# An edge gather and scatter-add: gathers ahead of the scatters paced by memsets, sums written into the rows they came from

## The chip, the cores and the metric

The kernel runs on one core of a Trainium2 chip. The metric is the device time of one execution in microseconds (us); the time before is the median of three runs. The profile is that of one further execution.

The engines are called by the short names of the profile: PE (TensorE matmul) and PEld (its weight load), DVE (VectorE), ACT (ScalarE), POOL (GpSimd, which here also issues every indirect DMA) and SP (SyncE, which here only issues DMAs). Times inside the profile count from the span's start.

## The reference

There are 100000 nodes of 128 float32 features, and 25000 edges, sorted by `dst`. The kernel adds to every node what its outgoing edges carry:

```
h   = maximum(layernorm(x), 0)
deg = number of edges with that src          (segment_sum of ones over src)
deg_inv = where(deg > 0, rsqrt(deg), 0)
for each edge e:  row = src[e], col = dst[e]
    norm   = deg_inv[row] * deg_inv[col]
    msg[e] = sum over b of comps[type[e], b] * (h[col] @ bases[b])     b = 0..3
    msg[e] = msg[e] * alpha[type[e]] * norm
out = x + segment_sum(msg, row)
```

## The kernel before

The edges are padded to 196 tiles of 128 edges, in 49 groups of 4 tiles. A tile's 128 gathered rows of x (one for each edge's `dst`) take `row(t)`, a [128, 128] float32 piece of the tensor `rows`, which has room for all 196 tiles. All orders are written out by hand; each engine has one instruction stream, and semaphores tie them.

- **Copy.** `out` must first be x. `copy` moves x to `out` in 50 pieces of 1 MB, two in flight, 4 from ACT's queue and 46 from SP's. Scatters add into `out`, so POOL waits for all of the copy before the first one.
- **Histogram.** PE counts the degrees with one-hot matmuls over the 196 tiles (L723); DVE makes the one-hots (L458, L459).
- **Looks.** For each tile PE looks up both degrees (`look`, L737, 8 matmuls), and DVE picks them out (`pick`, L481). DVE makes the one-hots for it in `turned_hots` (L475) from `edge_row`, a ring of broadcast rows that ACT's queue (at first SP's) loads.
- **Gathers.** `gather(t)` (L372) is an indirect DMA issued by POOL. ACT takes each group's mean and squares in `stats(g)` (L595 to L603), which waits for the landing of the group's four gathers.
- **Main loop,** 49 steps k of one group each. PE multiplies (L756), ACT takes the first of four terms (`first`, L641), DVE adds the other three (`combine`, L518), the last of which writes the message over `row(t)`.
- **Sums.** `add_same(t)` (PE, L764 and L766) adds up the messages of the same `src` inside a tile, and takes in what the tile before carries over. ACT evacuates it in `keep_sum(t)` (L651) into `acc`, a ring of 6 buffers.
- **Scatters.** POOL adds `acc` to `out` with an indirect DMA with add (L393). Scatter t waits for `keep_sum(t)` and for the landing of scatter t-2.

Three couplings matter for the change. `keep_sum(t)` waits until scatter t-6 has landed, because the ring has 6 buffers. `stats` at the end of step k goes as far as gathers that stand, in POOL's stream, ahead of the scatter `sums_until(k - 1)`; and `norms_in` on DVE needs the stats. POOL's stream itself is in this order:

1. gathers 0 to 55, each waiting for a share of the histogram;
2. gathers 56 to 107 (`FIRST_GATHERS` is 108), each waiting for a look or a product of PE (`pace`);
3. the wait for the copy;
4. the 196 scatters, with gathers 108 to 195 between them, seven to every ten scatters.

Sums are made in step k up to `sums_until(k)`, which is 5 (k - 2) up to step 10 and 4 k after it: in step 39 the sums 152 to 155, in step 42 the sums 164 to 167.

Of the kernel before, what the change touches and what calls it, by code (L numbers as in the profile page):

```python
# [5 lines left out]
ALU = mybir.AluOpType  # L6
ACT = mybir.ActivationFunctionType
# [6 lines left out]
P = 128  # L14
GROUP = 4
# [8 lines left out]
def build(nc, x, src, dst, edge_type, bases, comps, alpha, out):  # L24
    N, D = x.shape
    E = src.shape[0]
    R, B = comps.shape
    TILES = -(-E // P)
# [21 lines left out]
    FIRST_LOOK = 3  # L50
# [11 lines left out]
    TYPE_AT = [TILES - 1 - (TYPE_TILES - 1) * (TYPE_PARTS - 1 - i) for i in range(TYPE_PARTS)]  # L62
    TW = TYPE_TILES * P

    EDGE_RING = 4
    HOT_RING = 6
    TYPE_RING = 4
    SAME_RING = 3 * BATCH
    PART_RING = 7
    ACC_RING = 6  # L70


    def look_until(step):
# [6 lines left out]

    SUM_STEP, SUM_RATE = 3, 5


    HIST_GATHERS = 56
    LOOK_GATHERS = HIST_GATHERS + 4 * FIRST_LOOK * GROUP // 3
    FIRST_GATHERS = LOOK_GATHERS + 3 * GROUP * SUM_STEP


    def gathers_until(t):
        return min(TILES, FIRST_GATHERS + (7 * t + 9) // 10)  # L90

    def sums_until(step):
        return min(TILES, GROUP * max(0, step), max(0, step - SUM_STEP + 1) * SUM_RATE)
# [12 lines left out]
    def stats_until(step):  # L106
        return min(STATS_BEFORE + 2 * (step + 1), gathers_until(sums_until(step - 1)) // GROUP)
# [15 lines left out]
    with ExitStack() as ctx:  # L123
        def sb(name, shape, dt=F32):
            return ctx.enter_context(nc.sbuf_tensor(name, shape, dt))

        def sem(name):
            return ctx.enter_context(nc.semaphore(name))
# [24 lines left out]
        def row(t):  # L153
            return rows[:, t * D:(t + 1) * D]
# [27 lines left out]
        table = table_bits[:].bitcast(F16)  # L182
        edge_row = sb("edge_row", [P, EDGE_RING, 2, W], F16)
        turned_hot = sb("turned_hot", [P, 2, CHUNKS, 2 * W], F16)
# [23 lines left out]
        carried = sb("carried", [P, 2, BATCH])  # L208
        sum_scale = sb("sum_scale", [P, TILES])
        scatter_idx = sb("scatter_idx", [P, TILES], I32)  # L210
        acc = sb("acc", [P, ACC_RING, D])

        pst = ctx.enter_context(nc.psum_tensor("pst", [P, 8, BANK], F32))
        LOOK, TURNED, SUMS, PRODUCT = 0, 2, 3, 4
# [14 lines left out]
        row_table_ready = sem("row_table_ready")  # L229
        rows_stored = sem("rows_stored")  # L230
        idx_ready = sem("idx_ready")
        type_row_loaded = [sem(f"type_row_loaded{b}") for b in range(TYPE_RING)]
        edge_row_loaded = [sem(f"edge_row_loaded{r}") for r in range(EDGE_RING)]
        src_row_loaded = [sem(f"src_row_loaded{b}") for b in range(2)]
# [8 lines left out]
        look_ps = sem("look_ps")  # L243
# [11 lines left out]
        product_ready = sem("product_ready")  # L255
# [8 lines left out]
        scattered = [sem(f"scattered{b}") for b in range(2)]  # L264
# [9 lines left out]
        def load_edge_row(engine, g):  # L274
            if g >= EDGE_RING:
                engine.wait_ge(turned_hot_ready, g - EDGE_RING + 1)
            engine.dma_start(edge_row[:, g % EDGE_RING, :, :],
                             rows16_dram[0:2, g * W:(g + 1) * W].rearrange("(o k) e -> o k e", o=1)
                             .to_broadcast([P, 2, W])).then_inc(edge_row_loaded[g % EDGE_RING], 16)

# [58 lines left out]
        @block.gpsimd  # L339
        def _(pool):  # L340
            pool.iota(iota_i[:], [[1, CHUNKS * P]], base=0, channel_multiplier=0).then_inc(iota_ready, 1)
            pool.iota(chunk_i[:], [[P, CHUNKS]], base=0, channel_multiplier=1).then_inc(iota_ready, 1)
            pool.iota(spare_i[:], [[P, GROUP]], base=SPARE, channel_multiplier=1).then_inc(iota_ready, 1)
            pool.memset(ident[:], 0.0).then_inc(ident_cleared, 1)
            pool.memset(later[:, 0:P], 1.0).then_inc(ident_cleared, 1)
            pool.memset(later[:, P:2 * P], 1.0 / ONE).then_inc(ident_ready, 1)
            pool.wait_ge(ident_cleared, 2)
            pool.affine_select(out=ident[:], in_=ident[:], compare_op=ALU.not_equal, fill=1.0, base=0,
                               pattern=[[-1, P]], channel_multiplier=1).then_inc(ident_ready, 1)
            pool.affine_select(out=later[:, 0:P], in_=later[:, 0:P], compare_op=ALU.is_ge, fill=0.0, base=0,  # L350
                               pattern=[[1, P]], channel_multiplier=-1).then_inc(ident_ready, 1)

            def pace(t):
                if 0 < t < HIST_GATHERS:
                    pool.wait_ge(hot_used, t * TILES // HIST_GATHERS)
                elif HIST_GATHERS <= t < LOOK_GATHERS:
                    pool.wait_ge(look_ps, (t - HIST_GATHERS) * FIRST_LOOK * GROUP // (LOOK_GATHERS - HIST_GATHERS) + 1)
                elif LOOK_GATHERS <= t < FIRST_GATHERS:
                    tile, part = divmod(t - LOOK_GATHERS, 3)
                    if part == 0:  # L360
                        pool.wait_ge(product_ready, tile + 1)
                    else:
                        pool.wait_ge(look_ps, FIRST_LOOK * GROUP + 2 * tile + part)

            def gather(t):
                g = t // GROUP
                pace(t)
                if t == EARLY_TILE:
                    pool.wait_ge(hot_used, TILES)
                    pool.wait_ge(coef_ps, TYPE_PARTS)  # L370
                    pool.wait_ge(rows_stored, 16 * 4)
                pool.indirect_dma_start(row(t), None, x,  # L372
                                        bass.IndirectOffsetOnAxis(ap=dst_i[:, t:t + 1], axis=0)) \
                    .then_inc(row_gathered[g], 16)

            pool.wait_ge(idx_ready, 1)
            for t in range(FIRST_GATHERS):
                gather(t)
            gathered = FIRST_GATHERS

            pool.wait_ge(spare_filled, 16)
            for b in range(COPY_RING):
                pool.wait_ge(copied[b], 16 * (COPIES // COPY_RING))
            for t in range(TILES):
                for u in range(gathered, gathers_until(t)):
                    gather(u)
                gathered = gathers_until(t)
                if t % BATCH == 0:
                    pool.wait_ge(scatter_ready, t // BATCH + 1)
                if t >= 2:  # L390
                    pool.wait_ge(scattered[t % 2], 16 * (t // 2))
                pool.wait_ge(acc_ready, t + 1)
                pool.indirect_dma_start(out, bass.IndirectOffsetOnAxis(ap=scatter_idx[:, t:t + 1], axis=0),  # L393
                                        acc[:, t % ACC_RING, :], None, compute_op=ALU.add) \
                    .then_inc(scattered[t % 2], 16)

        @block.vector
# [192 lines left out]
        def _(act):  # L590
# [53 lines left out]
            def keep_sum(t):  # L644
                if t % BATCH == 0:
                    act.wait_ge(scatter_ready, t // BATCH + 1)
                act.wait_ge(sums_ps, t + 1)
                if t >= ACC_RING:
                    u = t - ACC_RING
                    act.wait_ge(scattered[u % 2], 16 * (u // 2 + 1))  # L650
                act.activation(acc[:, t % ACC_RING, :], pst[:, SUMS, 0:D], ACT.Copy, scale=sum_scale[:, t:t + 1]) \  # L651
                    .then_inc(acc_ready, 1)

            act.wait_ge(padded, 3)
# [41 lines left out]
            for t in range(sums_until(GROUPS - 1), TILES):  # L696
                keep_sum(t)

        @block.tensor
        def _(pe):  # L700
# [18 lines left out]
            for t in range(TILES):  # L719
                b = t % HOT_RING  # L720
                pe.wait_ge(hot_ready, t + 1)
                for c in range(CHUNKS):
                    last = pe.matmul(pst[:, HIST + c, 0:LO], hots[:, b, c * P:(c + 1) * P], hots[:, b, CHUNKS * P:],  # L723
                                     start=(t == 0), stop=(t == TILES - 1))
# [34 lines left out]
            def add_same(t):  # L759
                pe.wait_ge(same_ready, t + 1)  # L760
                pe.wait_ge(message_ready, t + 1)
                if t >= 1:
                    pe.wait_ge(acc_ready, t)
                last = pe.matmul(pst[:, SUMS, 0:D], same[:, t % SAME_RING, 0:P], row(t), start=True, stop=(t == 0))  # L764
                if t >= 1:
                    last = pe.matmul(pst[:, SUMS, 0:D], same[:, (t - 1) % SAME_RING, P:2 * P],  # L766
                                     acc[:, (t - 1) % ACC_RING, :], start=False, stop=True)
                last.then_inc(sums_ps, 1)

            pe.wait_ge(table_ready, CHUNKS)  # L770
# [5 lines left out]
            for k in range(GROUPS):  # L776
                if k + 1 < GROUPS:
                    turn(k + 1)
                for j in range(GROUP):
                    multiply(k * GROUP + j)  # L780
                    todo = sums_at(k, j)
                    for t in todo[:1]:
                        add_same(t)
                    for t in looks_at(k, j):
                        look(t)
                    for t in todo[1:]:
                        add_same(t)
            for t in range(sums_until(GROUPS - 1), TILES):
                add_same(t)
# [24 lines left out]
```

## Time and profile before

| | us |
|---|---|
| median of 3 runs (753.51 to 755.52) | 754.39 |
| the profiled execution | 752.15 |
| its span, first to last instruction | 750.2 |
| POOL busy | 540.3 |
| DVE busy | 596.4 |
| PE busy | 574.7 |
| ACT busy | 370.1 |

The span is 2 us shorter than the profiled execution's own time, and that one is 2.2 us under the median. The page cuts the span into 40 equal slices of 18.75 us and gives each engine's busy share in tenths. A row of the waits gives the idle time of an engine before a line, what ended it, how often, and the longest. Idle time of an engine that bounds nothing costs nothing.

### The profile page before, as it was taken

The page shows a single profiled execution, that of the slowest core. Times are in us where ns is not written, and L with a number is a line of the kernel's source. Part 1 is how long each engine was busy: PE and PEld are TensorE (multiplying, and loading weights), DVE is VectorE, ACT ScalarE, POOL GpSimd, SP SyncE. Part 2 cuts the span into 40 slices and gives each one's busy share as a digit, 9 for nine tenths or more (in the row PEclk, how much of TensorE's full clock was granted, in tenths as well). Part 3 has the DMA queues.
Part 4 walks back from the last instruction along what each step waited for, and adds up shares of the span by engine and source line. Part 5 has one row for each costly group of instructions (what it writes and reads, how often), then busy time and mean ns, then how long its engine had stood idle before and what let it go on. Part 6 is the DMA issues. An engine that isn't in the chain of part 4 may idle for free.

```text
span 750.2 us, 13642 instructions
## 1 busy us (share of the span) xinstructions
PE 574.7 (77%) x3922; PEld 406.0 (54%) x3922; DVE 596.4 (80%) x2624; ACT 370.1 (49%) x1494; POOL 540.3 (72%) x404
## 2 busy tenths in 40 slices
PE   4999985665676876987778788886797878888860
PEld 4666654443454645655556565655565656665430
DVE  7999995466775676886987899986998999998730
ACT  0345542244424678664545655645656534446530
POOL 3788886455555587778788888878878767767775
PEclk9999998687788899999998999999999999999995
DMA  8999999989833335444535455444455545544332
GB/s 272 287 326 339 331 361 323 319 296 327 307 101 81 70 54 122 79 92 69 109 52 100 92 86 95 96 81 95 82 95 96 92 78 78 86 57 82 35 36 25
DMA packets 56574, 108.89 MB, mean 145 GB/s; under 512 B 9339, under 2 KB 48264, under 8 KB 55684
## 3 DMA queue, kind: packets, MB, share of 16 engines
q0 software_dynamic: 34496, 25.72, 25.6%
q1 hardware_dynamic: 4416, 50.68, 18.7%
q10 hardware_dynamic: 17588, 31.62, 13.5%
q8 instruction: 32, 0.52, 0.3%
q14 instruction: 42, 0.34, 0.1%
HBM read 94.89 MB, written 64.61 MB: 213 GB/s over the span
## 4 chain that ended last, share of the span: by engine, by line
DVE 14%; DMA 13%; issue 10%; PE 9%; POOL 8%; ACT 7%; ACTq 0%; POOLq 0%
DMA out_dram<-acc,scatter_idx 11%; POOL out_dram L393 6%; DVE masked L481 4%; DVE part_sum L518 4%; PE pst L756 3%; PE pst L737 3%; DVE turned_hot L475 2%; POOL rows L372 2%; DVE same L537 2%; ACT acc L651 2%; DMA rows<-in_x_dram,dst_i 2%; DVE rows L518 2%; ACT scratch L603 2%; PE pst L764 1%; ACT scratch L595 1%
## 5 line engine op out<-in xcount | busy, mean ns | idle before, releaser
L393 POOL DMA_INDIRECT out_dram<-acc,scatter_idx x196 | 313.8, 1601 | 106.3 <-issue 53.7
L372 POOL DMA_INDIRECT rows<-in_x_dram,dst_i x196 | 224.4, 1145 | 96.4 <-issue 36.2
L737 PE MATMUL pst<-table_bits,turned_hot 128*128 128x198 f16 x1568 | 183.1, 267 | 84.0 <-DVE masked L481 61.1
L756 PE MATMUL pst<-bases_sb,h_turned 128*128 128x512 f32 x392 | 214.1, 629 | 0.0
L737 PEld LDWEIGHTS pst<-table_bits,turned_hot 128*128 128x128 f16 x1568 | 147.3, 105 | 113.6 <-issue 59.1
L518 DVE SCALAR_TENSOR_TENSOR part_sum<-pst,coef,part_sum 128x128 f32<-128x128 f32 x392 | 115.7, 343 | 96.2 <-ACT part_sum L641 89.3
L764 PEld LDWEIGHTS pst<-rows,same 128*128 128x128 f32 x392 | 73.0, 199 | 166.2 <-issue 152.1
L641 ACT ACTIVATE part_sum<-pst,coef 128x128 f32<-128x128 f32 x196 | 71.2, 363 | 183.4 <-PE pst L756 132.3
L481 DVE SCALAR_TENSOR_TENSOR masked<-iota_h,lo,pst 128x198 f32<-128x198 f16 x392 | 141.9, 415 | 20.9 <-PE pst L737 16.3
L764 PE MATMUL pst<-rows,same 128*128 128x128 f32 x392 | 82.7, 294 | 58.4 <-ACT acc L651 57.4
L651 ACT ACTIVATE acc<-pst,sum_scale 128x128 f32<-128x128 f32 x196 | 71.5, 365 | 58.5 <-DMA out_dram<-acc,scatter_idx 28.9
L723 PE MATMUL pst<-rows 128*128 128x198 f16 x784 | 88.5, 255 | 5.2 <-DVE rows L459 5.0
L475 DVE TENSOR_SCALAR turned_hot<-edge_row,chunk_id 128x1024 f16<-128x1024 f16 x196 | 86.8, 506 | 3.8 <-issue 3.8
L595 ACT ACTIVATE scratch<-rows 128x128 f32<-128x128 f32 x196 | 57.7, 297 | 64.8 <-DMA rows<-in_x_dram,dst_i 64.7
L537 DVE SCALAR_TENSOR_TENSOR same<-src_row,src_f,later 128x256 f32<-128x256 int32 x196 | 87.3, 478 | 0.4 <-issue 0.4
L766 PE MATMUL pst<-acc,same 128*128 128x128 f32 x390 | 78.4, 284 | 0.0
L603 ACT ACTIVATE scratch<-rows,less_mean 128x128 f32<-128x128 f32 x196 | 76.2, 390 | 1.6
L723 PEld LDWEIGHTS pst<-rows 128*128 128x128 f16 x784 | 58.9, 99 | 32.3 <-DVE rows L459 26.3
L458 DVE TENSOR_SCALAR rows<-iota_h,src_hi 128x512 f16<-128x512 f16 x196 | 67.5, 344 | 0.4 <-PE pst L723 0.2
L756 PEld LDWEIGHTS pst<-bases_sb,h_turned 128*128 128x128 f32 x392 | 63.1, 203 | 0.2
L766 PEld LDWEIGHTS pst<-acc,same 128*128 128x128 f32 x390 | 62.1, 200 | 0.0
L625 ACT ACTIVATE h<-rows,less_mean 128x128 f32<-128x128 f32 x196 | 61.9, 389 | 0.0
(71 smaller groups left out, 415.8 us busy)
## 6 DMA issues: line engine op xcount, KB each, us to landing
out_dram<-in_x_dram SPq DMA_DIRECT2D x46, 1000.0 KB
src_row<-src_rows ACTq DMA_DIRECT2D x25, 512.0 KB
edge_row<-edge_rows ACTq DMA_DIRECT2D x45, 256.0 KB
out_dram<-in_x_dram ACTq DMA_DIRECT2D x4, 1000.0 KB
rows<-in_x_dram,dst_i POOLq DMA_INDIRECT x196
out_dram<-acc,scatter_idx POOLq DMA_INDIRECT x196
rows<-edge_rows ACTq DMA_DIRECT2D x10, 175.0 KB
edge_row<-edge_rows SPq DMA_DIRECT2D x4, 256.0 KB
```

The lines of the kernel that those rows point to most:

```text
L372: pool.indirect_dma_start(row(t), None, x, bass.IndirectOffsetOnAxis(ap=dst_i[:, t:t + 1], axis=0)) \
L393: pool.indirect_dma_start(out, bass.IndirectOffsetOnAxis(ap=scatter_idx[:, t:t + 1], axis=0), acc[:, t % ACC_RING, :], None, compute_op=AL ...
L475: last = dve.tensor_scalar(turned_hot[:, g % 2, c, :], hi, chunk_id[:, c:c + 1], None, ALU.is_equal)
L481: last = dve.scalar_tensor_tensor(out=masked[:, 2 * (t % 2) + k, :], in0=iota_h[:, 0:LO], scalar=lo[:, k, t:t + 1], in1=pst[:, LOOK + t % ...
L518: dve.scalar_tensor_tensor(out=to, in0=pst[:, PRODUCT + t % 4, term * D:(term + 1) * D], scalar=coef[:, t, term:term + 1], in1=part_sum[:, ...
L537: dve.scalar_tensor_tensor(out=same[:, t % SAME_RING, 0:w], in0=src_row[:, b, j * P:j * P + w], scalar=src_f[:, t:t + 1], in1=later[:, 0:w ...
L603: last = act.activation(scratch[:, 1, j, :], row(t), ACT.Square, bias=less_mean[:, t:t + 1], accum_out=squares[:, t:t + 1])
L723: last = pe.matmul(pst[:, HIST + c, 0:LO], hots[:, b, c * P:(c + 1) * P], hots[:, b, CHUNKS * P:], start=(t == 0), stop=(t == TILES - 1))
L737: last = pe.matmul(pst[:, LOOK + t % 2, k * LO:(k + 1) * LO], turned_hot[:, g % 2, c, k * W + j * P:k * W + (j + 1) * P], table[:, c * LO: ...
L756: pe.matmul(pst[:, PRODUCT + t % 4, :], h_turned[:, g % 2, j, :], bases_sb[:].rearrange("d b f -> d (b f)"), start=True, stop=True).then_i ...
L764: last = pe.matmul(pst[:, SUMS, 0:D], same[:, t % SAME_RING, 0:P], row(t), start=True, stop=(t == 0))
L766: last = pe.matmul(pst[:, SUMS, 0:D], same[:, (t - 1) % SAME_RING, P:2 * P], acc[:, (t - 1) % ACC_RING, :], start=False, stop=True)
```

## The change

1. Gathers 56 to 119, 64 of them, no longer wait for PE. Ahead of each POOL runs two memsets of a [128, 40] tensor `beat`; the second waits for the end of the first, and the gather for the end of the second. `FIRST_GATHERS` becomes 120.
2. The other 76 gathers stand between the scatters, one to every two scatters (`t // 2`).
3. `keep_sum(t)` writes into `row(t)`, whose message PE has read by then. `acc` and the wait for scatter t-6 are gone; the carry (L766) and the scatter read `row`.
4. `EDGE_RING` becomes 5: SP loads five edge rows ahead of the copies and not four, and ACT's loads wait for a buffer of one group earlier.

The copy stays in whole pieces, as it was.

```diff
-    EDGE_RING = 4
+    EDGE_RING = 5
-    ACC_RING = 6
...
-    HIST_GATHERS = 56
-    LOOK_GATHERS = HIST_GATHERS + 4 * FIRST_LOOK * GROUP // 3
-    FIRST_GATHERS = LOOK_GATHERS + 3 * GROUP * SUM_STEP
+    HIST_GATHERS, FIRST_GATHERS = 56, 120

     def gathers_until(t):
-        return min(TILES, FIRST_GATHERS + (7 * t + 9) // 10)
+        return min(TILES, FIRST_GATHERS + t // 2)
...
-        acc = sb("acc", [P, ACC_RING, D])
+        beat = sb("beat", [P, 40])
...
+            beats = [0]
+
             def pace(t):
                 if 0 < t < HIST_GATHERS:
                     pool.wait_ge(hot_used, t * TILES // HIST_GATHERS)
-                elif HIST_GATHERS <= t < LOOK_GATHERS:
-                    pool.wait_ge(look_ps, (t - HIST_GATHERS) * FIRST_LOOK * GROUP // (LOOK_GATHERS - HIST_GATHERS) + 1)
-                elif LOOK_GATHERS <= t < FIRST_GATHERS:
-                    tile, part = divmod(t - LOOK_GATHERS, 3)
-                    if part == 0:
-                        pool.wait_ge(product_ready, tile + 1)
-                    else:
-                        pool.wait_ge(look_ps, FIRST_LOOK * GROUP + 2 * tile + part)
+                elif HIST_GATHERS <= t < FIRST_GATHERS:
+                    for _ in range(2):
+                        beats[0] += 1
+                        pool.memset(beat[:], 0.0).then_inc(beat_ended, 1)
+                        pool.wait_ge(beat_ended, beats[0])
...
                 act.wait_ge(sums_ps, t + 1)
-                if t >= ACC_RING:
-                    u = t - ACC_RING
-                    act.wait_ge(scattered[u % 2], 16 * (u // 2 + 1))
-                act.activation(acc[:, t % ACC_RING, :], pst[:, SUMS, 0:D], ACT.Copy, scale=sum_scale[:, t:t + 1]) \
+                act.activation(row(t), pst[:, SUMS, 0:D], ACT.Copy, scale=sum_scale[:, t:t + 1]) \
                     .then_inc(acc_ready, 1)
```

What stands on POOL from its first gather on, before the change (DMA `rows<-in_x_dram` is a gather; the names in brackets are the semaphores it waits for, `hot_used` the histogram's, `look_ps` and `product_ready` PE's):

```order
L372 DMA rows<-in_x_dram,dst_i 128x128 [waits idx_ready]
L372 DMA rows<-in_x_dram,dst_i 128x128 [waits hot_used] x55
L372 DMA rows<-in_x_dram,dst_i 128x128 [waits look_ps] x16
L372 DMA rows<-in_x_dram,dst_i 128x128 [waits product_ready]
L372 DMA rows<-in_x_dram,dst_i 128x128 [waits look_ps] x2
```

The same place after it:

```order
L368 DMA rows<-in_x_dram,dst_i 128x128 [waits idx_ready]
L368 DMA rows<-in_x_dram,dst_i 128x128 [waits hot_used] x55
L358 MEMSET beat 128x40
L358 MEMSET beat 128x40 [waits beat_ended]
L368 DMA rows<-in_x_dram,dst_i 128x128 [waits beat_ended]
```

The last three rows stand there 64 times, and nothing in them waits for another engine.

What stands on POOL between the scatters (DMA `out_dram<-acc` is a scatter; `scatter_ready` is its batch's indices) before the change, from scatter 4 on:

```order
L393 DMA out_dram<-acc,scatter_idx 100608x128 [waits acc_ready,scattered0]
L372 DMA rows<-in_x_dram,dst_i 128x128
L393 DMA out_dram<-acc,scatter_idx 100608x128 [waits acc_ready,scattered1]
L372 DMA rows<-in_x_dram,dst_i 128x128
L393 DMA out_dram<-acc,scatter_idx 100608x128 [waits acc_ready,scattered0]
L393 DMA out_dram<-acc,scatter_idx 100608x128 [waits acc_ready,scattered1,scatter_ready]
```

After it, among the later scatters, where the pattern is the same throughout:

```order
L368 DMA rows<-in_x_dram,dst_i 128x128
L389 DMA out_dram<-rows,scatter_idx 100608x128 [waits acc_ready,scattered0]
L389 DMA out_dram<-rows,scatter_idx 100608x128 [waits acc_ready,scattered1]
L368 DMA rows<-in_x_dram,dst_i 128x128
L389 DMA out_dram<-rows,scatter_idx 100608x128 [waits acc_ready,scattered0]
```

The gathers stand wider apart and go on longer: the last one stood ahead of scatter 125 and now stands ahead of scatter 152.

What ACT has at a late part of a step, before (`part_sum` is `first`, `acc` is `keep_sum`, `row_gathered28` the landing of group 28's gathers):

```order
L651 ACTIVATE acc<-pst,sum_scale 128x128 [waits scattered0,sums_ps]
L641 ACTIVATE part_sum<-pst,coef 128x128 [waits message_ready,product_ready]
L651 ACTIVATE acc<-pst,sum_scale 128x128 [waits scattered1,sums_ps]
L651 ACTIVATE acc<-pst,sum_scale 128x128 [waits scattered0,sums_ps]
L595 ACTIVATE scratch,row_sum<-rows 128x128 [waits row_gathered28]
```

and after:

```order
L644 ACTIVATE rows<-pst,sum_scale 128x128 [waits sums_ps]
L637 ACTIVATE part_sum<-pst,coef 128x128 [waits message_ready,product_ready]
L644 ACTIVATE rows<-pst,sum_scale 128x128 [waits sums_ps] x2
L591 ACTIVATE scratch,row_sum<-rows 128x128 [waits row_gathered28]
```

The wait for a scatter is gone from ACT; the wait for gathers has stayed.

## Rows read from the trace of the kernel before

**Rows 1.** The page: busy share in 40 slices, in tenths.
```profile
DVE  7999995466775676886987899986998999998730
POOL 3788886455555587778788888878878767767775
```

**Rows 2.** Stretches: length, then busy us (instructions) by engine, clock, DMA share, GB/s.
```profile
108.00:212.00 104.00, 63.23 (x387) 45.94 (x388) 66.67 (x293) 42.93 (x194) 55.16 (x55) 0.78 0.92 318
212.00:283.00 71.00, 51.15 (x296) 37.70 (x293) 48.49 (x218) 39.95 (x185) 47.55 (x34) 0.84 0.34 62
...
309.00:596.00 287.00, 229.46 (x1499) 166.44 (x1498) 246.69 (x1097) 164.03 (x637) 232.20 (x170) 0.98 0.48 88
596.00:679.00 83.00, 69.36 (x450) 49.52 (x450) 77.75 (x356) 36.56 (x111) 56.70 (x36) 1.00 0.49 80
```

**Rows 3.** Stretches, the scatters (L393) alone: busy us of POOL (count).
```profile
309.00:596.00 287.00, 161.25 (x101) 0.98 0.48 88
596.00:679.00 83.00, 56.70 (x36) 1.00 0.49 80
```

**Rows 4.** Stretches, the gathers (L372) alone: busy us of POOL (count).
```profile
309.00:596.00 287.00, 70.94 (x69) 0.98 0.48 88
```

**Rows 5.** Waits in 309 to 596: us, times, longest.
```profile
DVE part_sum L518 <- ACT part_sum L641: 34.8, 32, 5.5
...
ACT scratch L595 <- DMA rows<-in_x_dram,dst_i: 25.9, 7, 6.3
...
ACT acc L651 <- DMA out_dram<-acc,scatter_idx: 6.6, 5, 2.6
```

**Rows 6.** Timeline of ACT: start, duration, instruction, idle before it and its end.
```profile
335.16 0.37 ACT L651 ACTIVATE acc<-pst,sum_scale 128x128 f32<-128x128 f32 x1 [2.60 <-DMA out_dram<-acc,scatter_idx]
...
343.38 0.31 ACT L595 ACTIVATE scratch<-rows 128x128 f32<-128x128 f32 x1 [3.93 <-DMA rows<-in_x_dram,dst_i]
```

**Rows 7.** Timeline of POOL: gathers 55, 56 and 61, scatters 0, 20, 152, 195.
```profile
111.10 1.28 POOL L372 DMA_INDIRECT rows<-in_x_dram,dst_i  x1 [0.30 <-issue]
112.68 0.95 POOL L372 DMA_INDIRECT rows<-in_x_dram,dst_i  x1 [0.30 <-issue]
...
119.09 1.19 POOL L372 DMA_INDIRECT rows<-in_x_dram,dst_i  x1 [0.30 <-issue]
...
212.62 1.62 POOL L393 DMA_INDIRECT out_dram<-acc,scatter_idx  x1 [7.77 <-issue]
...
284.25 1.56 POOL L393 DMA_INDIRECT out_dram<-acc,scatter_idx  x1 [1.07 <-ACT acc L651]
...
653.02 1.55 POOL L393 DMA_INDIRECT out_dram<-acc,scatter_idx  x1 [1.61 <-DMA out_dram<-acc,scatter_idx]
...
742.16 1.55 POOL L393 DMA_INDIRECT out_dram<-acc,scatter_idx  x1 [0.30 <-issue]
```

**Rows 8.** Timeline of ACT: `first` of tiles 36, 136, 168 (steps 9, 34, 42).
```profile
309.38 0.35 ACT L641 ACTIVATE part_sum<-pst,coef 128x128 f32<-128x128 f32 x1
...
596.42 0.35 ACT L641 ACTIVATE part_sum<-pst,coef 128x128 f32<-128x128 f32 x1
...
678.75 0.37 ACT L641 ACTIVATE part_sum<-pst,coef 128x128 f32<-128x128 f32 x1 [3.29 <-DVE same L537]
```

**Rows 9.** Timeline of POOL at the start: its memsets.
```profile
0.40 0.12 POOL L802 MEMSET const-uint8-127<- 128x1 uint8 x1
...
1.72 0.19 POOL L345 MEMSET later<- 128x128 f32 x1
1.86 0.19 POOL L346 MEMSET later<- 128x128 f32 x1
2.08 0.41 POOL L348 TENSOR_SCALAR_AFFINE_SELECT ident<-ident 128x128 f32<-128x128 f32 x1
```

**Rows 10.** DVE's `turned_hots` (L475): its row at 117.79, and a stretch of them.
```profile
117.79 1.67 DVE L475 TENSOR_SCALAR turned_hot<-edge_row,chunk_id 128x1024 f16<-128x1024 f16 x4
...
112.00:212.00 100.00, 13.71 (x33) 0.77 0.90 312
```

More of the change, by code:

```diff
@@ L231, in build @@
         idx_ready = sem("idx_ready")
+        beat_ended = sem("beat_ended")
         type_row_loaded = [sem(f"type_row_loaded{b}") for b in range(TYPE_RING)]
@@ L393, in _ @@
                 pool.indirect_dma_start(out, bass.IndirectOffsetOnAxis(ap=scatter_idx[:, t:t + 1], axis=0),
-                                        acc[:, t % ACC_RING, :], None, compute_op=ALU.add) \
+                                        row(t), None, compute_op=ALU.add) \
                     .then_inc(scattered[t % 2], 16)
@@ L766, in add_same @@
                     last = pe.matmul(pst[:, SUMS, 0:D], same[:, (t - 1) % SAME_RING, P:2 * P],
-                                     acc[:, (t - 1) % ACC_RING, :], start=False, stop=True)
+                                     row(t - 1), start=False, stop=True)
                 last.then_inc(sums_ps, 1)
```

## The prediction

> **What bounds the kernel now.** I read the slices first, then stretches cut where the slices change, then the waits, then single instructions on POOL and ACT. The slices show no engine full from end to end, but after the copy DVE and POOL are the two that come near it [rows 1], so the question is which of them sets the pace in which stretch.
>
> From 309 to 596 us, steps 9 to 33, it is POOL. It issued 101 scatters in 161.25 us and 69 gathers in 70.94 us, 1.60 and 1.03 us each [rows 3, 4], and between two of them lie 0.30 us even where nothing is awaited [rows 7]. So a scatter takes 1.90 us of POOL's stream and a gather 1.33 us, and 101 x 1.90 + 69 x 1.33 = 283.7 us of the 287 are POOL's: 99%. DVE is busy for 246.69 of them, 86% [rows 2]. The other engines feel it through the two couplings: ACT stands still for a scatter that has to land (6.6 us) and for gathers (25.9 us), and DVE waits 34.8 us for ACT in turn [rows 5]; one wait of each kind is shown [rows 6]. A step took (596.42 - 309.38) / 25 = 11.5 us [rows 8].
>
> From 596 to 679 us, steps 34 to 41, the gathers are over, POOL is busy for 56.70 us and DVE for 77.75 of 83, 94% [rows 2, 3]. A step took (678.75 - 596.42) / 8 = 10.3 us [rows 8]. That is the pace of the loop without POOL in its way.
>
> At the end POOL sets the pace again: looks are over, the loop's steps become short, and the scatters are left. From scatter 152 at 653.02 to scatter 195 at 742.16 there are 43 intervals in 89.1 us, 2.07 each, and 8.0 us later the span ends [rows 7]. Before 283 us POOL bounds nothing: scatter 20 at 284.25 waited for ACT's sum [rows 7], and the granted clock of 0.78 and 0.84 of full speed [rows 2], between its two levels of 1.2 and 2.4 GHz, and PE and DVE waiting for each other are what make those steps long.
>
> So the end is the time of scatter 152 plus 97 us, and the change is worth what it does to scatter 152.
>
> **The beats.** Gathers 56 to 119 lose their waits for PE and get two memsets each. Gather 55 ended at 112.4 us [rows 7]. A 128x40 memset lies between the 128x1 of 0.12 us and the 128x128 of 0.19 us, so 0.14 us; the first instruction on POOL that waited for a memset, at 2.08, started 0.17 us after that memset's end at 1.91 [rows 9], which bounds the wait for a beat. The gather itself is 0.95 us at its shortest [rows 7] and 1.03 us in the mean [rows 4]. One period is then at least 0.14 + 0.14 + 0.30 + 0.95 = 1.53 us (no wait for the beats) and at most 0.30 + 0.14 + 0.17 + 0.14 + 0.17 + 0.30 + 1.03 = 2.25 us (both waits beside the 0.30 us that a DMA has ahead of it anyway, and 0.30 ahead of the first memset too). I take 1.90, the middle, as a wait that is over before the 0.30 us are costs nothing more. 64 x 1.90 = 122 us, so the last gather ends at 234 (bounds 210 and 256), and the first scatter, at 212.62 now [rows 7], starts there: 21 us later. In the same time there are 12 gathers more done.
>
> Is the late start hidden? POOL has 20 scatters and 10 gathers to do before scatter 20: 20 x 1.90 + 10 x 1.33 = 51 us, so scatter 20 goes at 285.6, against 284.25 now. It has just caught up, and the 21 us are paid for by the waiting that POOL does now before 283 us. That holds up to a start at about 234; each us after that costs up to a us. Neither ACT nor PE waits for a scatter any longer, so nothing else is held up by the late start, and all groups of which stats are taken before step 8 are among the 120.
>
> One rule weighs on this. The gather at 119.09 took 1.19 us, and it lay beside four `turned_hots` that ran from 117.79 to 119.46 [rows 7, 10]; `turned_hots` are 13.71 of 100 us there [rows 10]. The Trainium skill's page "SBUF — State Buffer", section "Who interferes with whom", says that a `tensor_scalar` in a mode that uses both ports locks GpSimd out for the whole instruction. By that rule 14% of the 128 memsets would wait half of a 0.4 us operation, about 4 us in all, and the first scatter would start at 238 and not 234; the trace agrees as far as the gather at 119.09 goes, and no row shows a memset beside such an operation.
>
> **Fewer gathers between the scatters.** From scatter 20 to scatter 152 POOL has 132 scatters and 66 gathers: 132 x 1.90 + 66 x 1.33 = 338.6 us, and at the 98.9% that it reached, 342.6. From 285.6 that gives scatter 152 at 628, against 653.0. This is the bound by POOL.
>
> The bound by the loop: step 9 starts at 309.4 as now (steps 6 to 8 took 13 to 15 us before POOL was full, and POOL needs 5 x 1.90 + 2.5 x 1.33 = 12.8 us for their five sums). Thirty steps of 10.3 to 10.4 us give step 39 at 620, and scatter 152 followed the start of its step by 4 us, so 624. The two bounds are 4 us apart. Two chains that are so near to each other don't give the larger of the two: stats still wait for gathers that stand right behind the scatter of the step before, so a late scatter still holds ACT, though only in every second step (half a group per step, seven tenths now). I add 5 us for this and take scatter 152 at 633, 20 us earlier. The bounds of this term: 624, and 650 if the beats take their upper price (start at 256, then 51.3 + 342.6 us with no waiting).
>
> **The sums in the rows.** L651 costs the same to another address. The 6.6 us (28.9 us in the whole span) that ACT waited for a scatter go, but in the stretch that POOL fills they were only POOL's time showing on ACT; I count nothing for them alone. Nothing new waits: PE's second matmul waits for the same evacuation as before.
>
> **Five edge rows.** One load of 256 KB moves from ACT's queue to SP's, ahead of the copies. The copy needs it neither more nor less in sum; as ACT issues a load in the same step as before, nothing comes earlier from group 5 on. Nothing; if the copy ended 1 us later, that would still be before 234.
>
> **The sum.** Scatter 152 at 633 instead of 653, then 43 x 2.07 + 8 = 97 us as now: span 730, 20 under the 750.2. From the profiled execution (752.15) this gives 732, and from the median of the runs, 2.2 us above that execution, 754.4 - 20 = 734.4. I predict 734.
>
> **Rivals.**
> *The loop holds the pace by itself.* Then fewer gathers only make POOL idle. For it: DVE is already 86% busy, PE 80%, DVE waits for ACT 32 times [rows 2, 5], and stats interrupt ACT in a step. Against it: steps 34 to 41 are 10.3 us each. The excess of 25 x 1.2 = 30 us from 309 to 596 fell on 69 / 4 = 17 groups of stats. If all of it came with the stats' own work, the 66 / 4 = 16.5 groups that remain would bring 29 us of it again: step 39 at 309.4 + 309 + 29 = 647, and the time at 752. With two thirds of it, 19 us, step 39 comes at 638 and the time is 742.
> *The beats are dear (the other side).* Everything hangs on the wait of an engine for its own memset. Scatter 152 at 653 or later needs a start of the scatters at 653 - 51.3 - 342.6 = 259, so a period of (259 - 112.4) / 64 = 2.29 us: from there on the kernel is slower. That is just above my upper bound. The beats would have to take (2.29 - 0.30 - 0.95) / 2 = 0.52 us each, where I read 0.14 + 0.17 = 0.31. At 1 us each the period is 3.25, the scatters start at 320 and the time is 320 + 394 + 97 + 4 = 815. The 0.17 us are from one place only, and the locking rule above works in this direction.
> *More than forecast.* With no ring, ACT never waits for a landing, and if both bounds were reached together, the loop at 10.0 a step and the tail at the 1.95 of two scatters per landing, scatter 152 comes at 613 to 620 and the end at 717 to 724.
>
> **How the numbers follow.** Forecast, 722 to 745: 0.66. The loop holds the pace, 745 to 757: 0.14, of which half is within 0.3% or slower. Beats dear, above 757: 0.09. More than forecast, 712 to 722: 0.09; the rest, 0.02, is slower for a reason that I don't see. A measurement tells about 0.3%, 2.3 us, from no change. So faster 0.82, same 0.07, slower 0.11, and for 8 in 10 the range is 721 to 749.
>
> **What would show it.** The first scatter at 234, with a period of 1.90 us from gather to gather before it; scatter 20 at about 285; POOL still above 93% of its stream from there to scatter 152, at 633; steps 9 to 38 at 10.7 us; waits of ACT for gathers fewer than now, and none for scatters; from scatter 152 to the end 97 us. A first scatter after 259, or steps of 11.5 us with POOL idle between them, would make me wrong.

## The result, and the profile after

The changed kernel takes 735.44 us (median of 4 runs, 728.89 to 740.92) against 754.95 us for the kernel before in the same comparison (4 runs): the ratio is 0.9705, with a 95% interval of 0.9628 to 0.9782. Executions of any kernel can fall in a slower state, with a lower granted clock and a longer time; the ratios leave them out, here the 740.92. Two later comparisons of the same pair, on two other chips, gave 0.9686 (0.9617 to 0.9754) and 0.9710 (0.9659 to 0.9761). 734 us was forecast. The profiled execution took 728.89 us with a span of 727.1 us; it is the fastest of its kernel, some 6 us under the median and so its times run a little early. In the profiles of the two later comparisons scatter 152, at 632.46 below, came at 637.0 and 633.4.

The page of the changed kernel, busy share in 40 slices of 18.2 us; the rows answer to [rows 1]:

```profile
DVE  7999998465875676589999999989999999987820
POOL 3888888877877667688787778888787888877885
```

The same stretches as in [rows 2], moved to where the changed kernel's steps lie (columns: length, busy us and instructions of PE, PEld, DVE, ACT, POOL, then clock, DMA share, GB/s):

```profile
108.00:212.00 104.00, 63.13 (x402) 45.60 (x402) 71.26 (x314) 42.88 (x189) 82.19 (x188) 0.84 0.93 311
212.00:277.00 65.00, 46.22 (x264) 34.52 (x264) 42.45 (x192) 38.55 (x181) 45.81 (x37) 0.82 0.38 68
...
307.00:624.00 317.00, 270.24 (x1798) 197.56 (x1798) 293.74 (x1317) 183.20 (x673) 254.23 (x179) 0.99 0.49 92
```

From 307 to 624 us (steps 9 to 38) DVE is now busy for 93%, where it was 86%; POOL did 120 scatters and 59 gathers there, 254.23 us which with 0.30 us ahead of each make 97% of the stretch. A step takes (623.61 - 307.52) / 30 = 10.5 us, where it took 11.5.

POOL's timeline at the first beats: gather 55, and then each time the two memsets in one row and the gather that waited for them. The last row is a pair that took longer.

```profile
109.97 1.28 POOL L368 DMA_INDIRECT rows<-in_x_dram,dst_i  x1 [0.30 <-issue]
111.25 0.34 POOL L358 MEMSET beat<- 128x40 f32 x2
111.85 0.96 POOL L368 DMA_INDIRECT rows<-in_x_dram,dst_i  x1 [0.27 <-POOL beat L358]
112.81 0.34 POOL L358 MEMSET beat<- 128x40 f32 x2
113.42 0.96 POOL L368 DMA_INDIRECT rows<-in_x_dram,dst_i  x1 [0.27 <-POOL beat L358]
114.38 0.34 POOL L358 MEMSET beat<- 128x40 f32 x2
114.98 0.98 POOL L368 DMA_INDIRECT rows<-in_x_dram,dst_i  x1 [0.27 <-POOL beat L358]
115.97 0.74 POOL L358 MEMSET beat<- 128x40 f32 x2
```

An undisturbed period is 1.57 us. From gather 56 at 111.85 to gather 119 at 215.30 there are 63 periods in 103.45 us, 1.64 each. POOL at scatters 0, 20, 152 and 195, as in [rows 7]:

```profile
216.56 1.62 POOL L389 DMA_INDIRECT out_dram<-rows,scatter_idx  x1 [0.30 <-issue]
...
278.21 1.57 POOL L389 DMA_INDIRECT out_dram<-rows,scatter_idx  x1 [1.82 <-ACT rows L644]
...
632.46 1.82 POOL L389 DMA_INDIRECT out_dram<-rows,scatter_idx  x1 [0.30 <-issue]
...
718.71 1.55 POOL L389 DMA_INDIRECT out_dram<-rows,scatter_idx  x1 [0.30 <-issue]
```

The scatters start 4 us later than before, scatter 20 comes 6 us earlier and waits for ACT's sum as it did, and scatter 152 comes 20.6 us earlier (653.02 before). The waits from 307 to 624 us, against [rows 5]:

```profile
DVE part_sum L514 <- ACT part_sum L637: 19.5, 29, 3.5
...
ACT scratch L591 <- DMA rows<-in_x_dram,dst_i: 10.9, 8, 2.8
```

ACT waits less than half as long for gathers, and for scatters not at all; DVE waits 19.5 us for ACT and not 34.8.

### The profile page after: what moved, and what is told of

The parts are those of the page before. It is cut to its first block, busy times and chain, and to the rows that moved or that the text cites. A ratio compares the mean times of both kernels' runs of the same rounds, so it can differ in the third digit from the quotient of the medians.

```text
span 727.1 us, 13608 instructions
## 1 busy us (share of the span) xinstructions
PE 565.0 (78%) x3922; PEld 402.3 (55%) x3922; DVE 592.9 (82%) x2624; ACT 372.6 (51%) x1494; POOL 560.1 (77%) x532
## 4 chain that ended last, share of the span: by engine, by line
DVE 31%; PE 20%; ACT 14%; issue 12%; DMA 11%; POOL 10%; SPq 1%; ACTq 1%; POOLq 0%; DVEq 0%
POOL out_dram L389 8%; PE pst L749 7%; PE pst L730 6%; DVE part_sum L514 6%; DVE masked L477 6%; DVE rows L454 5%; ACT scratch L599 5%; DMA edge_row<-edge_rows 4%; ACT scratch L591 4%; DVE turned_hot L471 3%; DVE same L533 3%; DVE rows L455 3%; DVE rows L514 3%; DMA rows<-in_x_dram,dst_i 3%; DMA out_dram<-rows,scatter_idx 3%
## 5 line engine op out<-in xcount | busy, mean ns | idle before, releaser
L389 POOL DMA_INDIRECT out_dram<-rows,scatter_idx x196 | 312.2, 1593 | 87.8 <-issue 47.2
L730 PE MATMUL pst<-table_bits,turned_hot 128*128 128x198 f16 x1568 | 179.6, 263 | 82.6 <-DVE masked L477 66.0
L730 PEld LDWEIGHTS pst<-table_bits,turned_hot 128*128 128x128 f16 x1568 | 145.0, 104 | 110.7 <-issue 59.4
L757 PEld LDWEIGHTS pst<-rows,same 128*128 128x128 f32 x392 | 74.0, 198 | 139.7 <-issue 127.7
L757 PE MATMUL pst<-rows,same 128*128 128x128 f32 x392 | 81.3, 290 | 36.7 <-ACT rows L644 31.2
L644 ACT ACTIVATE rows<-pst,sum_scale 128x128 f32<-128x128 f32 x196 | 71.6, 365 | 38.3 <-PE pst L759 24.7
L471 DVE TENSOR_SCALAR turned_hot<-edge_row,chunk_id 128x1024 f16<-128x1024 f16 x196 | 84.5, 494 | 8.0 <-DMA edge_row<-edge_rows 8.0
L759 PE MATMUL pst<-rows,same 128*128 128x128 f32 x390 | 78.1, 283 | 0.0
L454 DVE TENSOR_SCALAR rows<-iota_h,src_hi 128x512 f16<-128x512 f16 x196 | 69.1, 353 | 0.1
L759 PEld LDWEIGHTS pst<-rows,same 128*128 128x128 f32 x390 | 61.9, 200 | 0.0
```

The lines of the kernel that those rows point to most:

```text
L471: last = dve.tensor_scalar(turned_hot[:, g % 2, c, :], hi, chunk_id[:, c:c + 1], None, ALU.is_equal)
L730: last = pe.matmul(pst[:, LOOK + t % 2, k * LO:(k + 1) * LO], turned_hot[:, g % 2, c, k * W + j * P:k * W + (j + 1) * P], table[:, c * LO: ...
```

## The experiments

All ratios are to the kernel before, in runs on the same chip. The theory was that of the prediction: after the copy POOL's stream is nearly full, the change takes work out of it between scatter 20 and scatter 152, and the late start of the scatters is hidden. The rivals: that the ring's wait on ACT was the cost, that the number of gathers ahead of the copy's end is all that counts, that the loop sets the pace by itself.

**The sums in the rows alone** (the kernel before with part 3 of the change).

```diff
-                if t >= ACC_RING:
-                    u = t - ACC_RING
-                    act.wait_ge(scattered[u % 2], 16 * (u // 2 + 1))
-                act.activation(acc[:, t % ACC_RING, :], pst[:, SUMS, 0:D], ...
+                act.activation(row(t), pst[:, SUMS, 0:D], ...
```

> The kernel before with one part of the change: keep_sum writes into the rows, no ring acc and no wait for scatter t-6; gathers paced and placed as before. Theory (the gain is that POOL has fewer gathers between the scatters): POOL is as full as before between 309 and 596 us, so within 2 us of before, up to 4 us faster in the tail, where scatters went every 1.94 us after the change and every 2.00 before. Rival (ACT's waits for a scatter's landing, 28.9 us in the span of before, were the cost): 10 us or more faster, near 742.

Measured: 744.66 us against 744.8, 0.9986 (0.9948 to 1.0024), no difference. The 28.9 us that ACT waited for scatters were no cost of their own. That they were POOL's time seen on ACT, as the prediction has it, fits; what ACT waited for in their place is not shown, as the one profile of this kernel is that of its longest execution.

**The gathers alone** (parts 1 and 2 of the change on the kernel before; ring and its wait kept, four edge rows).

```diff
-    FIRST_GATHERS = LOOK_GATHERS + 3 * GROUP * SUM_STEP
+    HIST_GATHERS, FIRST_GATHERS = 56, 120
-        return min(TILES, FIRST_GATHERS + (7 * t + 9) // 10)
+        return min(TILES, FIRST_GATHERS + t // 2)
```

and the two memsets in `pace`.

> The kernel before with the other large part alone: gathers 56 to 119 behind two memsets each, the other 76 one to every two scatters; acc with its 6 buffers and its wait stays, 4 edge rows. Theory: most of the 20 us, 736 to 740, since POOL's work between scatter 20 and scatter 152 is 338 us in place of 366. Rival (the gain needs ACT free of the ring): 745 to 755.

Measured: 729.15 us against 744.8, 0.9807 (0.9742 to 0.9871). That is a gain of 15.6 us, and the expectation's 736 to 740 stood for 14 to 18; but this chip's kernel before was 744.8 us, the changed kernel had not run on it, and so it was open whether a per cent was missing. It was run again beside the changed kernel:

> The changed kernel once more, as the measure for the next three on this chip: about 0.970 of the kernel before.

> The gathers' part of the change alone again (ring acc of 6 buffers and its wait kept, 4 edge rows), this time beside the changed kernel on one chip. Theory: within 3 us of the changed kernel, since the ring's wait only shows when POOL is late. Rival (the ring's removal is worth 1% once POOL is no longer full): 6 to 9 us slower than the changed kernel.

Measured: the changed kernel 730.31 us, 0.9710 (0.9659 to 0.9761); the gathers alone 729.97 us, 0.9710 (0.9651 to 0.9769). The gathers are the whole of the change; the ring's removal and the fifth edge row add nothing that these runs can tell.

**No beats** (the changed kernel with `range(0)` in `pace`).

> The changed kernel with no memset ahead of gathers 56 to 119, so that they follow each other on POOL in about 1.26 us, and the last ends near 192 in place of 216. The scatters wait for the copy then, to about 212. Theory (POOL's start of the scatters has slack up to about 234): the same as the changed kernel, 732 to 738. Rival (gathers bunched under the copy delay the edge rows that the looks need, and the first steps come later): 5 us or more slower than the changed kernel.

Measured: 731.42 us, 0.980 (0.9735 to 0.9864), on the same chip as the 0.9807 of the gathers alone. The last gather of the row ahead was at 193.6 us, the scatters started at 209.2 and not 216.6, and scatter 20 (278.6) and scatter 152 (634.1) came no earlier for it. The changed kernel itself did not run on this chip, so this compares with the gathers alone, 729.15 us. The beats neither help nor cost as far as that shows; the start has slack, and gathers bunched under the copy do no harm: tile 36 starts at 308.1 as in the changed kernel (307.5).

**Five beats** (`range(5)`).

> The changed kernel with five memsets ahead of each of gathers 56 to 119 in place of two. Two took 0.34 us with a gap of 0.27 behind them, so each more should take about 0.2 us, the period go from 1.64 to 2.2 us, and the scatters start at 111 + 64 x 2.2 = 254 in place of 217. Theory (slack to 234, then a us for a us at most): about 10 to 20 us slower than the changed kernel, 745 to 755. Rival (the loop sets the pace, and POOL catches up later): within 4 us of the changed kernel.

Measured: 759.08 us, 1.0192 (1.0139 to 1.0245). It comes out slower than the kernel before. The direction is the expected one, the size is not: about 30 us slower than the gathers alone on the same chip (729.15), where 10 to 20 against the changed kernel were expected. POOL at scatters 0, 20 and 152, and ACT at tile 36:

```profile
256.63 1.69 POOL L389 DMA_INDIRECT out_dram<-rows,scatter_idx  x1 [0.30 <-issue]
...
311.35 1.57 POOL L389 DMA_INDIRECT out_dram<-rows,scatter_idx  x1 [1.32 <-DMA out_dram<-rows,scatter_idx]
...
661.89 1.82 POOL L389 DMA_INDIRECT out_dram<-rows,scatter_idx  x1 [0.30 <-ACT rows L644]
```

```profile
307.88 0.35 ACT L637 ACTIVATE part_sum<-pst,coef 128x128 f32<-128x128 f32 x1
```

The loop came to tile 36 as early as ever, and lost its time afterwards, by the wait of stats for gathers that stand behind late scatters (34.8 us from 277 to 603 us). From scatter 0 to scatter 152 POOL was hardly ever short of sums (about 2 us beyond the 0.30 us that every DMA has ahead of it), and took 405.3 us. The forecast's prices give 51.3 + 342.6 = 393.9 for it.

**The old density** (the changed kernel with seven gathers to ten scatters).

```diff
-        return min(TILES, FIRST_GATHERS + t // 2)
+        return min(TILES, FIRST_GATHERS + (7 * t + 9) // 10)
```

> The changed kernel itself, as the measure for the other three on this chip. About 0.975 of the kernel before; scatter 152 near 632 us and 95 us from there to the end.

> The changed kernel with seven gathers to every ten scatters, as before the change, in place of one to two; the 76 gathers behind the copy are then over ahead of scatter 109. The work of POOL up to scatter 152 is the same as in the changed kernel. Theory (POOL and the loop bound in turn, and what counts is that neither idles): POOL takes 89 x 1.9 + 66 x 1.33 = 257 us from scatter 20 to 109, to 540, and the loop can't catch up, at 10.3 us a step: scatter 152 at 645 to 653, 15 to 20 us slower than the changed kernel. Rival (only the number of gathers ahead of the copy's end counts): the same as the changed kernel.

Measured: the changed kernel 731.25 us, 0.9686 (0.9617 to 0.9754); with the old density 749.0 us, 0.9976 (0.9945 to 1.0008). This is the experiment that decides: 120 gathers ahead, beats, no ring, the same work on POOL before scatter 152, and the gain is gone (its interval leaves 0.55% at most, where the changed kernel gains 3.1%). Stretches of it before and after its gathers end:

```profile
305.00:540.00 235.00, 189.82 (x1208) 138.59 (x1208) 199.86 (x889) 139.23 (x554) 188.99 (x137) 0.94 0.48 88
540.00:642.00 102.00, 89.25 (x592) 65.07 (x590) 95.46 (x429) 44.79 (x132) 65.76 (x42) 0.98 0.45 79
```

Up to 540 us POOL is busy for 80% (and 0.30 us ahead of each of its 137 DMAs make it 98%) and DVE for 85%; then DVE for 94% and POOL for 64% (77% with its 0.30 us). Each waits for the other in turn. Scatter 152 comes at 644.2, step 39 at 641.8; this profile is of the fastest execution of its kernel, 744.47 us. The waits of POOL from scatter 109, where the gathers are over, to scatter 152 (537 to 644.5 us) show where its time goes:

```profile
POOL out_dram L389 <- ACT rows L644: 14.6, 7, 5.3
...
POOL out_dram L389 <- DMA out_dram<-rows,scatter_idx: 11.8, 9, 2.0
```

and between the same two scatters of the changed kernel (518 to 632.6 us), where 22 gathers stand among them:

```profile
POOL out_dram L389 <- DMA out_dram<-rows,scatter_idx: 3.6, 5, 1.2
POOL out_dram L389 <- ACT rows L644: 0.3, 1, 0.3
```

So the old density takes 20 us longer from scatter 20 to scatter 109 (260.0 us against 239.6), in which it puts 18 gathers more, and gets back only 7 from there to scatter 152 (107.3 against 114.6), because POOL then waits for sums and landings. Its steps 9 and 10 have two groups of stats each (14.8 and 16.0 us, where the changed kernel took 11.7 and 10.3), but this is not what held it: in the 260.0 us POOL was idle for only 7 beside its 0.30 us per DMA.

**All gathers ahead** (`FIRST_GATHERS = 196`).

> The changed kernel with all 196 gathers ahead of the scatters, 140 of them behind two memsets each; the scatters start at 111 + 140 x 1.64 = 341 us, with no gather between them. Nothing in the loop waits for a scatter. Theory: the loop runs at its own pace, 10.3 us a step or less, and POOL needs 152 x 1.9 = 289 us to scatter 152, at 630, so within 5 us of the changed kernel, from 5 faster to 3 slower; ACT's waits for gathers are gone after 300 us and show what the loop needs alone. Rival (the late start costs as in the run with five beats): 20 us or more slower.

Measured: 779.84 us, 1.0342 (1.0279 to 1.0405), 49 us slower than the changed kernel: the rival's figure came. The theory's fell on both counts. First, scatters alone don't go every 1.90 us while the loop runs. Scatters 0 and 152:

```profile
349.13 1.67 POOL L389 DMA_INDIRECT out_dram<-rows,scatter_idx  x1 [0.30 <-issue]
...
692.47 1.55 POOL L389 DMA_INDIRECT out_dram<-rows,scatter_idx  x1 [0.30 <-issue]
```

152 scatters take 343.3 us, 2.26 each, and the waits of POOL say why (349 to 650 us):

```profile
POOL out_dram L389 <- DMA out_dram<-rows,scatter_idx: 46.9, 33, 3.6
```

A scatter waits for the landing of the one before the last. Second, the loop was not at its fastest with all rows there, though scatter 152 came 43 us after the start of step 39 (649.2) and so did not wait for it; tiles 52 and 56 (steps 13 and 14) start 13.6 us apart:

```profile
365.85 0.35 ACT L637 ACTIVATE part_sum<-pst,coef 128x128 f32<-128x128 f32 x1
...
379.45 0.35 ACT L637 ACTIVATE part_sum<-pst,coef 128x128 f32<-128x128 f32 x1
```

From step 11 to step 16 every step takes 13.6 to 13.7 us: these have two groups of stats each, 6.2 us of ACT in one piece from 373.27 on, in which no `first` is done. The same is true of steps 5 to 8 of the changed kernel (14.7 to 15.9 us each); step 9, with one group, took 11.7.

**Four edge rows** (the changed kernel with `EDGE_RING = 4`).

> The changed kernel with 4 buffers for edge rows as before. Theory: ACT issues the loads in the same steps, so no difference, within 2 us. Rival (the fifth row, there before the looks begin, is what brought tile 0 of the loop from 140 to 131 us): 5 to 9 us slower.

Measured: 731.11 us, 0.9713 (0.9655 to 0.9771), beside 731.25 of the changed kernel. No difference. Tile 0 of the loop started at 132.4 us, so its 131.6 in the changed kernel against 140.2 before is not the fifth row's doing; with the rows part alone it was 133.9. It differs between executions.

**Stats apart** (the changed kernel, with one of two groups moved to the middle of the step). This follows from the 13.6 us.

```diff
+                    if j == 1 and stats_until(k) - done_stats == 2:
+                        stats(done_stats)
+                        done_stats += 1
```

> The changed kernel, but where a step has two groups of stats (steps 0 to 8), ACT does one after the second tile and one at the step's end in place of both at the end. Theory (two groups of 3.1 us each in a row on ACT make such a step 13.6 us, where one makes it 10 to 11): steps 5 to 9 get 2 us shorter each and tile 36 starts near 298 in place of 308; 5 to 10 us faster than the changed kernel. Rival (PE's clock and the looks set these steps): no difference.

Measured: 721.07 us, 0.9609 (0.9558 to 0.9661), 9 us faster than the changed kernel on the same chip and the best of all. Tile 36, and scatters 0 and 152:

```profile
278.83 0.35 ACT L637 ACTIVATE part_sum<-pst,coef 128x128 f32<-128x128 f32 x1
```

```profile
216.76 1.85 POOL L389 DMA_INDIRECT out_dram<-rows,scatter_idx  x1 [0.30 <-issue]
...
621.72 1.57 POOL L389 DMA_INDIRECT out_dram<-rows,scatter_idx  x1 [0.30 <-issue]
```

The loop was at tile 36 29 us earlier, not 10, and only 9 of them reached the median. Steps 5 to 8 took 12.0 to 12.2 us each and gave 13 us; steps 0 to 4, which have two groups of stats as well, took 100 us in all where they took 115 (111 to 118 in the profiles of all other kernels in which they stand together). The granted clock in 216 to 278 us was 0.97, where the changed kernel had 0.83; both rows:

```profile
216.00:278.00 62.00, 49.55 (x323) 35.95 (x323) 53.90 (x242) 45.36 (x211) 49.43 (x36) 0.97 0.45 80
```

```profile
216.00:278.00 62.00, 44.01 (x252) 32.56 (x251) 40.02 (x178) 39.55 (x184) 42.64 (x31) 0.83 0.40 70
```

Then POOL was the bound: 405.0 us from scatter 0 to scatter 152, the same as the 405.3 with five beats, and the loop was held when it ran too far ahead:

```profile
324.79 0.31 ACT L591 ACTIVATE scratch<-rows 128x128 f32<-128x128 f32 x1 [9.77 <-DMA rows<-in_x_dram,dst_i]
```

**Stats apart and 132 gathers ahead.**

> As the run before, with 132 gathers ahead of the scatters in place of 120, so that they start near 235 and POOL has 12 gathers fewer between them. Theory (landings of two scatters take 4.5 us while the loop runs, so that a gather beside them costs POOL 0.6 us and not 1.33, while the start comes 12 x 1.6 = 19 us later): no gain, 0 to 8 us slower than the run before. Rival (POOL is as dear as forecast, 1.33 a gather): 3 to 6 us faster than the run before.

Measured: 738.16 us, 0.9835 (0.9778 to 0.9891), 17 us slower than the run before. The direction was the theory's, the size twice the upper end of what was expected. Scatters 0 and 152:

```profile
238.16 1.62 POOL L389 DMA_INDIRECT out_dram<-rows,scatter_idx  x1 [0.31 <-issue]
...
638.25 1.77 POOL L389 DMA_INDIRECT out_dram<-rows,scatter_idx  x1 [2.11 <-DMA out_dram<-rows,scatter_idx]
```

The start is 21.4 us later and POOL's 152 scatters with 64 gathers take 400.1 us and not 405.0; together 16.5 us, which is nearly the whole difference. The 12 gathers fewer are those behind scatter 128, and there POOL runs short: from scatter 109 to scatter 152 it waited 10.6 us for landings and 7.6 for sums. With POOL full from its first scatter on, there is no slack for a late start at all.

Set side by side, from scatter 0 to scatter 152:

| kernel | gathers between | scatter 0 | scatter 152 | us |
|---|---|---|---|---|
| all gathers ahead | 0 | 349.1 | 692.5 | 343.3 |
| stats apart, 132 ahead | 64 | 238.2 | 638.2 | 400.1 |
| stats apart | 76 | 216.8 | 621.7 | 405.0 |
| five beats | 76 | 256.6 | 661.9 | 405.3 |
| the changed kernel | 76 | 216.6 | 632.5 | 415.9 |
| old density | 76 | 218.3 | 644.2 | 425.9 |
| before | 88 | 212.6 | 653.0 | 440.4 |

In the first four POOL, with the landings that it waits for, is the bound: it waits for sums for at most 6 us in all beyond the 0.30 us of each DMA. The changed kernel is 11 us above the two that have 76 gathers as well, 7 of them before scatter 20 (61.6 us from scatter 0 to 20, 54.7 with five beats), where POOL waits for sums.

## Why the prediction was right

**What bounds the kernel, and where.** Right. POOL between steps 9 and 33, the loop up to step 41, POOL at the end; the old density shows that the alternation itself cost the time, since it brings all of it back with the same work. Of what the prediction named as a sign, POOL's share of its stream from scatter 20 to scatter 152 was 96% ((211.5 + 70.1 + 198 x 0.30) of 354.3 us; above 93% was forecast).

**The beats.** The direction is right, the term was mis-sized: a period of 1.64 us and not 1.90, so the scatters start at 216.6 and not 234. Two memsets take 0.34 us together, so the wait between them is no 0.17 us (one memset takes 0.13, which leaves 0.08), and only 0.27 us lie behind the second, within the 0.30 us that a DMA has ahead of it anyway. The chosen value was the middle of bounds whose lower one, 1.53, was nearly right. On the rule of the Trainium skill's page "SBUF — State Buffer", section "Who interferes with whom", the trace agrees: 12 of the 64 pairs of memsets lay beside `turned_hots` and took 0.57 us in the mean, the other 52 took 0.34; 12 x 0.23 = 2.8 us in all, where about 4 had been worked out from the rule. Three of the 12 took no longer than the others.

**The late start is hidden.** Right: scatter 20 waited for ACT's sum, and without beats nothing was gained. How far it is hidden was mis-sized. The forecast had the slack last to a start at 234; scatter 20's sum came at 278.2, and 51.3 us ahead of it is 227. The forecast put the point from which the kernel is slower than before at a start of 259; five beats started at 256.6 and were already 14 us slower than the kernel before on that chip, which puts the point at about 242. With 405 us from scatter 0 to scatter 152 and the profile of the kernel before, from another chip, it is 653 - 405 = 248.

**Fewer gathers between the scatters.** The direction and the size are right, and that scatter 152 came at 632.5 for 633 is in part luck: two errors met each other, and in the two later profiles it came at 637.0 and 633.4. POOL's bound from scatter 20 on is 350.5 us (five beats) and 351.8 (stats apart), not 342.6. With five beats the 198 DMAs there fill 342.0 us with their 0.30 us each (212.24 + 70.31 + 59.4), 3.4 more than the 338.6 of the forecast, and the other 8.5 are waits, half of them for landings. Against that stands the earlier scatter 20, 278.2 for 285.6 (the forecast's own terms, 234 + 51.3, give 285.3). The 5 us that were added for two bounds close to each other fit: the changed kernel took 354.3 us. What the forecast's sum does not say is that less work for POOL is not enough: with the old density POOL has 132 scatters and 62 gathers there, four gathers fewer than in the changed kernel, and takes 367.3 us, as long as the kernel before with its 74 (368.8). The gain came from where the gathers stand; the forecast had this only in its two bounds 4 us apart. Steps 9 to 38 take 10.5 us, 10.7 had been forecast.

**The sums in the rows, the fifth edge row.** Right, both are worth nothing that was measured.

**The end.** 97 us were forecast from scatter 152 on, 94.6 were measured; 43 intervals of 2.01 us in place of 2.07. This is the spread of executions: the two later profiles of the changed kernel have 2.07 and 2.05, and 97.5 and 96.7 us to the end.

**The rivals.** That the loop holds the pace by itself is refuted by the steps of 10.5 us; but a part of it was true in another place. Two groups of stats in one piece did lengthen steps 5 to 8, which the forecast had put down to the clock and to PE and DVE waiting for each other. The dear beats exist as a mechanism, at five and not at two.

## What to carry to other kernels

When one engine's stream is nearly full in one stretch and starved in the next, look at where its optional work stands in the order: the same 76 gathers spread over 152 scatters instead of 109 were worth 18 us here, while 12 more of them ahead at the old density, the beats and a removed buffer wait were worth nothing. Whether the wider spacing needs the 12 gathers ahead is not shown. ACT's wait for late scatters was no cost of its own here; before removing such a wait, ask what is late behind it. Work that is moved ahead of a full stream delays all of it: it is free up to the slack that the stream still has, and costs about a us for a us beyond: here a start 40 us later (five beats) cost 30, as 10 were slack.

## What the runs showed of the hardware

- A scatter of 128 rows with add, waiting for the landing of the one before the last, goes every 2.26 us while the loop runs, and every 1.94 us in the same kernel's tail (scatter 152 at 692.47 to scatter 195 at 776.0), though POOL itself needs 1.57 + 0.30 us; what in the loop makes the landings later is not shown. One gather to two scatters makes it 5.33 us for the three (405.3 us for 76 of them), so such a gather costs 0.8 us by this estimate, not the 1.33 us of its own time.
- A wait of POOL for its own memset costs under 0.1 us: a memset takes 0.13 us, two with the wait between them take 0.34, five with four waits 0.90.
- PE's granted clock from 216 to 278 us went from 0.83 to 0.97 when nothing but ACT's order was changed (0.83 and 0.86 in the two later profiles of the changed kernel, 0.97 in the other one with stats apart). PE was idle less there (busy for 49.55 of 62 us against 44.01, with 323 instructions against 252), so some of the 29 us that the loop gained may be the clock's; the runs don't separate the two.
- Left open: whether stats apart without beats is faster still. POOL is the bound there from the first scatter on, and without beats the scatters started 7 us earlier. It wasn't run. Nor was the kernel with 108 gathers ahead and one gather to two scatters, which would tell the spacing from the number ahead for good.
